# Linear attention and gated FFN: orders of their own for the first tile on three engines, casts of the value weights on GpSimd, a tiny first activation

## The chip, the cores and the metric

One core of a Trainium2 chip. The metric is the device time of one execution in microseconds (us), the median of several runs.

## The reference, cut

```python
x = _layernorm(x + attn(x, Wq, Wk, Wv, Wo))
x = _layernorm(x + ffn(x, ...))
# attn: x is 1 x 4096 x 512; 16 query heads, 4 key/value heads of 128
q, k = rope(x @ Wq.T), rope(x @ Wk.T); v = x @ Wv.T
qf, kf = elu(q) + 1, elu(k) + 1
# per head, over the sequence:
state = state + k_s[:, None] * v_s[None, :]; z = z + k_s
out = (q_s @ state) / (q_s . z + 1e-6);  out @ Wo.T
# ffn: Walsh-Hadamard transforms around gate/up (2048) and down, silu(gate) * up, scales
```

## The kernel before, in words

The program runs in three stages: attention over 8 tiles of 512 tokens, the output projection with the first norm over 32 chunks of 128, and the FFN. All products of float32 are made of three matmuls of upper and lower parts: `hi = round(x)`, `lo = x - hi`, and `hi*hi + hi*lo + lo*hi`. So each weight block and each operand needs an upper part (a copy, mostly on ScalarE) and a lower part (a subtraction, mostly on VectorE) before TensorE can use it.

In the attention stage each engine has a list of events written out by hand (`ORDER_PE`, `ORDER_ACT`, `ORDER_DVE`, `ORDER_POOL`, `ORDER_SP`); `events_in` reads them and `bodies` runs them in three places: "start" (the events marked with ', which belong to tile 0), a hardware loop over 7 tiles, and "end". An event is a letter, a key/value group g (0 to 3) and an index c:

- J (TensorE): projection of the key (c = 0) or query c of group g, 12 matmuls of 128x512, for all 512 tokens, into one of three banks `pj` that J, V, T and D share in turn. V: values of 128 tokens, 12 matmuls. T: transposes of the key features. D: denominators. C: scores of a chunk. U: numerators of a chunk. Z: the state's update.
- S (ScalarE): swaps the halves of J's result into `tb` (two instructions of 64x512). M (VectorE): result times cosines. I (GpSimd): `tb` times sines. R (VectorE): their sum. X (ScalarE): exponential. E (VectorE): the feature; it frees the bank of J. L: upper part of the feature on ScalarE (`Qh`) and lower part on GpSimd (`Ql`).
- W, K, A, N: upper parts on ScalarE and lower parts on VectorE of values, transposed keys, scores and state. G (GpSimd): the two causal selects on the scores' parts. H: parts of the x tile. Q (VectorE): running sum of the key features. P: query feature times that sum. O, Y: copies out of PSUM. B, S, O, Y on SyncE: loads of x and tables, stores.

In the first tile the weights come in too: 24 pieces of 128x512 (`piece`, in the order in which TensorE first uses them: J00 to J04, V0 to V3, J10 to J14, J20 to J24, J30 to J34). SyncE loads them one after the other (`load_piece`), `pieces_hi` makes the upper parts and counts them in `wa_hi`, `pieces_lo` makes the lower parts and counts them in `wa_lo`; TensorE's J or V waits for that count, and the first J of the second tile (J21) for all 24. Before, ScalarE makes all upper parts, and the table `ahead` says how many pieces are made ahead of each S on ScalarE and ahead of each M on VectorE: 3 ahead of the first, then 2 ahead of each of the next ten. TensorE waits by the order of the list: J02 needs E00 for its bank, J04 needs E01, V0 needs E02 and all four value pieces, J10 E03, V1 E04, J11 the lower part W1, J13 E10, J14 E11, V2 E12, V3 E13, and Z01 the lower part N01.

Of the kernel before, what the change touches and what calls it, by code (L numbers as in the profile page):

```python
# [10 lines left out]
ACT = mybir.ActivationFunctionType  # L11
# [77 lines left out]
NW = H + KV + DC  # L89
# [9 lines left out]
def jobs_before(kind, a, b, d, where):  # L99
# [15 lines left out]
                return found  # L115
    return found

LAST_PE = """  # L120
# [32 lines left out]
def phases(nc, xT, wq, wk, wv, cosT, sinT, x, wo, su, consts, wd, sd, wsd, wg, wu, wsg, wsu, num_d, den_d, rden_d, x1_d, x2_d, wd_d, out):  # L153
# [9 lines left out]
    with ctx:  # L163
        def sem(name):
            return ctx.enter_context(nc.semaphore(name))
# [134 lines left out]
        had_done = sem("had_done")  # L300
        had_free = sem("had_free")
        x2_out = sem("x2_out")
        f_in, sc_in, sd_ready = sem("f_in"), sem("sc_in"), sem("sd_ready")
        f_step, f_hi, f_lo, f_mm, f_w, f_out = sem("f_step"), sem("f_hi"), sem("f_lo"), sem("f_mm"), sem("f_w"), sem("f_out")
        w_in, wd_in = [sem(f"wc_in{i}") for i in range(XR)], [sem(f"wd_in{i}") for i in range(WDS)]
# [87 lines left out]
        order = list(first)  # L393
# [10 lines left out]

        def bodies(eng, name, body):

            body(-1, [e for e in EVENTS[name] if e[3] == 1], "start")
            with eng.Fori(0, NM - 1) as m:
                body(m, EVENTS[name], "middle")
            body(NM - 1, LAST_TILE.get(name, [e for e in EVENTS[name] if e[3] == 0]), "end")  # L410

        ahead = {(0, 0): 3}
        left = NW - 4
        for e in [e for e in EVENTS["ACT"] if e[0] == "S" and e[3]][1:]:
            ahead[e[1:3]] = min(2, left)
            left -= ahead[e[1:3]]
        assert left == 0

        def upto(m, d, per_tile, i):  # L420

# [291 lines left out]
        def _(act):  # L713
# [192 lines left out]
            def pieces_hi(n):  # L906
                for i in [next(pieces) for _ in range(n)]:
                    _, raw_w, hi, _ = piece(i)
                    act.wait_ge(wa_in[i], 16)
                    nc.scalar.activation(hi, raw_w, ACT.Copy).then_inc(wa_hi, 1)  # L910

            def body(m, events, where):
                for kind, g, c, d in events:
                    u = g * NCH + c
                    r = g * (G + 1) + c
                    if kind == "S" and where == "start":
                        pieces_hi(ahead.get((g, c), 0))
                    if kind == "S":
                        bank = pj[job_bank("J", g, c)]
                        act.wait_ge(j_done, upto(m, d, NR, r))  # L920
# [44 lines left out]
                    if where == "end":  # L965
                        between(kind, g, c)

            pieces = iter(range(NW))
            act.wait_ge(zeroed, 5)
            pieces_hi(1)  # L970
            bodies(act, "ACT", body)
# [14 lines left out]
        def _(dve):  # L986
# [225 lines left out]
            def pieces_lo(n):  # L1212
                for i in [next(pieces) for _ in range(n)]:
                    _, raw_w, hi, lo = piece(i)
                    dve.wait_ge(wa_hi, i + 1)
                    nc.vector.tensor_tensor(lo, raw_w, f32(hi), ALU.subtract).then_inc(wa_lo, 1)

            def body(m, events, where):
                for kind, g, c, d in events:
                    u = g * NCH + c  # L1220
                    r = g * (G + 1) + c
                    if kind == "M" and where == "start":
                        pieces_lo(ahead.get((g, c), 0))
                    if kind in "MRE":
                        bank = pj[job_bank("J", g, c)]
                    if kind == "M":
# [90 lines left out]
        def _(pool):  # L1317
# [66 lines left out]
            def row_root(k, t):  # L1384
                i = k * NCH + t
                pool.wait_ge(lnc_step, i * 3 + 3)
                nc.gpsimd.tensor_tensor(crstd[:, :], cve[:, :], neghalf[:, :], ALU.pow).then_inc(rc_done, 1)

            def body(m, events, where):
                for kind, g, c, d in events:  # L1390
                    u = g * NCH + c
                    r = g * (G + 1) + c
                    if kind == "I":
                        if r == 0:
                            pool.wait_ge(cs_in, m * 32 + (d * 32 + 32))
                        pool.wait_ge(shifted, upto(m, d, NR, r))
                        nc.gpsimd.tensor_tensor(tb[c][:, :], tb[c][:, :], sinb[:, :], ALU.mult).then_inc(sin_done, 1)  # L1397
                    elif kind == "L":
                        pool.wait_ge(hi_done, upto(m, d, NR, r))
                        nc.gpsimd.tensor_tensor(Ql[g % 2][:, c, :], (tb[c] if c else Kf)[:, :], f32(Qh[g % 2][:, c, :]),  # L1400
                                                ALU.subtract).then_inc(lo_done, 1)
                    elif kind == "G":
                        pool.wait_ge(sc_free, upto(m, d, NU, u))
                        nc.gpsimd.sem_inc(passed, 1)
                        for a in (Ah[u % 2], Al[u % 2]):

                            ins = nc.gpsimd.affine_select(out=a[:, :, :], in_=a[:, :, :], compare_op=ALU.is_ge, fill=0.0,  # L1407
                                                          base=0, pattern=[[0, G], [1, CH]], channel_multiplier=-1)
                        ins.then_inc(a_ready, 1)
# [3 lines left out]
            nc.gpsimd.memset(carry[:], 0.0).then_inc(zeroed, 1)  # L1413
            nc.gpsimd.memset(minus1[:], -1.0).then_inc(zeroed, 1)
            nc.gpsimd.memset(onesd[:], 1.0).then_inc(zeroed, 1)
            nc.gpsimd.memset(neghalf[:], -0.5).then_inc(zeroed, 1)

            for s, tile in ((j_done, NR), (v_done, NCH), (t_done, KV), (dn_done, KV), (shifted, NR), (cos_done, NR),
                            (sin_done, NR), (rot_done, NR), (exp_done, NR), (f_done, NR), (hi_done, NR), (lo_done, NR),
# [25 lines left out]
        def _(sp):  # L1445
# [171 lines left out]
                sp.dma_start(xst[:, c, :], xT[0, :, c, :]).then_inc(xst_in[c], 16)  # L1617
            sp.dma_start(pr[-1][:, :], xT[0, :, DC - 1, :]).then_inc(xst_in[DC - 1], 16)
            load_piece(1)
            sp.dma_start(cosb[:, :], cosT[:, 0:MT]).then_inc(cs_in, 16)  # L1620
            sp.dma_start(sinb[:, :], sinT[:, 0:MT]).then_inc(cs_in, 16)
            sp.dma_start(identb[:, :], consts[:, 0:P]).then_inc(c_in, 16)
            for i in range(2, NW):
                load_piece(i)
            sp.dma_start(had[:, :], consts[:, P:2 * P]).then_inc(mat_in, 16)
            bodies(sp, "SP", body)
# [109 lines left out]
```

## Time and profile before

| | us |
|---|---|
| median of 3 runs | 2312.55 (2310.44 to 2315.09) |
| the profiled execution | 2315.09 |
| its span | 2313.4 |
| TensorE busy | 2251.4 (97%) |
| VectorE busy | 1826.6 (79%) |
| ScalarE busy | 1274.0 (55%) |
| GpSimd busy | 1128.7 (49%) |

The profile is one execution on the chip. Its timeline rows give the start of an instruction, its time, engine, source line, operation, and in brackets how long the engine had been idle before it and what ended the wait. PE is TensorE, DVE VectorE, ACT ScalarE, POOL GpSimd, SPq the queue of SyncE.
### The profile page before, as it was taken

Reading aid. Unit: us, or ns where it says so; the run is one execution under the profiler, and the core shown is the slowest. Engines: PE = TensorE matmul, PEld = TensorE weight load, DVE = VectorE, ACT = ScalarE, POOL = GpSimd, SP = SyncE. Lnnn points to the kernel's source line nnn. Section 1 sums busy time; section 2 is a strip of 40 time slices with the busy share of each in tenths; the row PEclk is TensorE's granted clock in tenths of the full one; section 3 lists DMA queues with packets and bytes.
Section 4 is the critical chain, followed back from the end, with each engine's and each line's share of the span. In section 5 each row is a group of like instructions: output and inputs, shape, how many; then the busy total and the mean of one; then the engine's idle time right before and its main releaser. Section 6 shows DMA issues by size and latency. Waiting matters only on the chain.

```text
span 2313.4 us, 32819 instructions
## 1 busy us (share of the span) xinstructions
PE 2251.4 (97%) x10209; PEld 1820.0 (79%) x10209; DVE 1826.6 (79%) x2452; ACT 1274.0 (55%) x2285; POOL 1128.7 (49%) x1002
## 2 busy tenths in 40 slices
PE   7999999999999999899999989999999999999998
PEld 5778777787878786787777768888888888888886
DVE  7877777878686868687887896787888788878877
ACT  6666666666676767233334455454445554554543
POOL 4677677767676767355544633321242133303321
PEclk9999999999999999999999999999999999999999
DMA  4010111111020115677767541323233322222313
GB/s 154 36 65 37 68 37 68 51 49 68 32 73 32 68 71 190 235 250 251 248 229 262 190 139 62 123 78 114 78 100 94 116 85 94 91 82 82 104 61 101
DMA packets 132701, 252.75 MB, mean 109 GB/s; under 512 B 44576, under 2 KB 45344, under 8 KB 122880
## 3 DMA queue, kind: packets, MB, share of 16 engines
q1 hardware_dynamic: 132608, 251.60, 32.3%
q8 instruction: 48, 0.79, 0.1%
q14 instruction: 45, 0.37, 0.1%
HBM read 188.11 MB, written 63.44 MB: 109 GB/s over the span
## 4 chain that ended last, share of the span: by engine, by line
PE 70%; issue 11%; POOL 9%; DVE 6%; ACT 2%; DMA 1%; SPq 0%; POOLq 0%; ACTq 0%; DVEq 0%
PE pj L548 17%; PE pj L629 11%; PE pnum L629 6%; PE pj L643 5%; PE psc L629 5%; PE pst L629 4%; PE psc L643 4%; PE pj L558 3%; PE pnum L643 3%; PE psc L579 3%; PE pnum L597 3%; PE pnum L600 3%; PE pst L643 2%; POOL fa L1337 1%; PE pst L586 1%
## 5 line engine op out<-in xcount | busy, mean ns | idle before, releaser
L1364 POOL TENSOR_TENSOR wcs<-wcr 128x256 f32<-128x256 f32 x64 | 67.3, 1051 | 514.1 <-DVE wcl L1106 504.2
L1397 POOL TENSOR_TENSOR tb<-tb,sinb 128x512 f32<-128x512 f32 x160 | 224.3, 1402 | 91.5 <-ACT tb L925 90.7
L548 PE MATMUL pj<-xah,wqh 128*128 128x512 f32 x512 | 203.3, 397 | 4.4 <-DVE Kf L1242 2.7
L478 PE MATMUL pj<-woh,oh 128*128 128x512 f32 x512 | 202.8, 396 | 1.7 <-issue 1.7
L1400 POOL TENSOR_TENSOR Ql<-tb,Qh 128x512 fp32r<-128x512 f32 x128 | 170.5, 1334 | 68.8 <-ACT Qh L934 68.8
L478 PE MATMUL pj<-woh,ol 128*128 128x512 f32 x512 | 200.4, 391 | 0.0
L478 PE MATMUL pj<-wol,oh 128*128 128x512 f32 x512 | 200.2, 391 | 0.0
L548 PE MATMUL pj<-xal,wqh 128*128 128x512 f32 x512 | 200.2, 391 | 0.0
L548 PE MATMUL pj<-xah,wql 128*128 128x512 f32 x512 | 200.1, 391 | 0.0
L1230 DVE TENSOR_TENSOR pj<-pj,cosb 128x512 f32<-128x512 f32 x160 | 111.2, 695 | 69.1 <-ACT tb L925 68.5
L629 PE MATMUL pj<-xch,wch 128*128 128x512 f32 x384 | 150.2, 391 | 8.5 <-DVE xcl L1112 6.2
L924 ACT ACTIVATE tb<-pj 64x512 f32<-64x512 f32 x160 | 95.5, 597 | 112.7 <-PE pj L548 108.7
L1407 POOL TENSOR_SCALAR_AFFINE_SELECT Ah<-Ah 128x512 fp32r<-128x512 f32 x128 | 102.0, 797 | 109.8 <-DVE Al L1271 109.1
L629 PE MATMUL pj<-xcl,wch 128*128 128x512 f32 x384 | 149.4, 389 | 0.0
L629 PE MATMUL pj<-xch,wcl 128*128 128x512 f32 x384 | 149.4, 389 | 0.0
L1256 DVE TENSOR_TENSOR pr<-tb,zc 128x512 f32<-128x512 f32 x128 | 140.5, 1112 | 1.2 <-PE pj L572 1.2
L1234 DVE SCALAR_TENSOR_TENSOR pj<-pj,tb 128x512 f32<-128x512 f32 x160 | 110.9, 693 | 35.1 <-POOL tb L1397 33.8
L928 ACT ACTIVATE tb<-pj,minus 128x512 f32<-128x512 f32 x160 | 110.5, 691 | 44.2 <-DVE pj L1234 42.6
L1320 POOL TENSOR_TENSOR rstd<-ve,neghalf 128x1 f32<-128x1 f32 x32 | 48.6, 1520 | 174.5 <-DVE ve L1000 174.5
L548 PEld LDWEIGHTS pj<-xah,wqh 128*128 128x128 f32 x512 | 96.7, 189 | 32.3 <-issue 7.5
L1177 DVE SCALAR_TENSOR_TENSOR tha<-tha,ga 128x512 f32<-128x512 f32 x64 | 53.6, 838 | 80.8 <-ACT tha L869 80.6
L839 ACT ACTIVATE wdh<-wdr 128x512 fp32r<-128x512 f32 x123 | 77.1, 627 | 70.3 <-PE pj L643 34.8
(258 smaller groups left out, 7070.5 us busy)
## 6 DMA issues: line engine op xcount, KB each, us to landing
num_scratch<-no SPq DMA_DIRECT2D x128, 256.0 KB, 2.4
nt<-num_scratch SPq DMA_DIRECT2D x32, 1024.0 KB, 5.4
rb<-rden_scratch SPq DMA_DIRECT2D x32, 1024.0 KB, 6.3
wdr<-wd_scratch SPq DMA_DIRECT2D x128, 256.0 KB, 3.3
wcr<-in_wg SPq DMA_DIRECT2D x64, 256.0 KB, 2.8
wcr<-in_wu SPq DMA_DIRECT2D x64, 256.0 KB, 3.1
xst<-in_xT SPq DMA_DIRECT2D x34, 256.0 KB, 3.7
xr<-in_x SPq DMA_DIRECT2D x32, 256.0 KB, 5.6
```

The source lines that it names most:

```text
L478: last = nc.tensor.matmul(py[s][:, :], a[s][:, h, :], b[:, h, :], start=(h == 0 and i == 0), stop=(h == H - 1 and i == 2))
L548: last = nc.tensor.matmul(bank[:, :], w[:, b, :], x[:, b, :], start=(k == 0), stop=(k == 11))
L629: last = nc.tensor.matmul(bank[:, :], a[n % 2][:, w, c, :], b[i][:, c, :], start=(start and k == 0), stop=(k == 5), skip_group_check=True)
L643: last = nc.tensor.matmul(result_banks(k)[t][:, :], a[:, tok], b[:, :], start=(f == 0 and i == 0), stop=(f == FB - 1 and i == 2))
L924: nc.scalar.activation(tb[c][0:64, :], bank[64:128, :], ACT.Copy)
L928: nc.scalar.activation(tb[c][:, :], pj[job_bank("J", g, c)][:, :], ACT.Exp, bias=minus1[:, 0:1]).then_inc(exp_done, 1)
L1230: nc.vector.tensor_tensor(bank[:, :], bank[:, :], cosb[:, :], ALU.mult).then_inc(cos_done, 1)
L1234: nc.vector.scalar_tensor_tensor(out=bank[:, :], in0=bank[:, :], scalar=1.0, in1=tb[c][:, :], op0=ALU.add, op1=ALU.add).then_inc(rot_done, 1)
L1256: nc.vector.tensor_tensor(pr[c - 1][:, :], tb[c][:, :], zc[:, :], ALU.mult).then_inc(z_product, 1)
L1397: nc.gpsimd.tensor_tensor(tb[c][:, :], tb[c][:, :], sinb[:, :], ALU.mult).then_inc(sin_done, 1)
L1400: nc.gpsimd.tensor_tensor(Ql[g % 2][:, c, :], (tb[c] if c else Kf)[:, :], f32(Qh[g % 2][:, c, :]), ALU.subtract).then_inc(lo_done, 1)
L1407: ins = nc.gpsimd.affine_select(out=a[:, :, :], in_=a[:, :, :], compare_op=ALU.is_ge, fill=0.0, base=0, pattern=[[0, G], [1, CH]], channel ...
```

## The change

Three tables give ScalarE, VectorE and GpSimd orders of their own for the start body; the loop's orders stay. In them `wN` makes the next N pieces (upper parts on ScalarE, lower parts on VectorE), `vN` the next N upper parts of value weights on GpSimd, counted by a semaphore of their own. The table `ahead` is gone. TensorE's and SyncE's lists are the same, but the load of the third piece (J02) is issued ahead of the cosines. ScalarE's first instruction is an activation of one column that makes the constant -0.5 (a memset on GpSimd before) and waits for no load; the load of the activation table stands ahead of it.

```diff
+FIRST_DVE = """
+H0 H1 H2 H3 w2 M00 R00 w1 E00 M01 w1 R01 E01 M02 w1 R02 w3 E02 M03 R03 w1 Q0 E03 M04 R04 W0 E04 M10 w2 R10 W1
...
-            body(-1, [e for e in EVENTS[name] if e[3] == 1], "start")
+            body(-1, [e[:3] + (1,) for e in FIRST_TILE[name]] if name in FIRST_TILE else
+                 [e for e in EVENTS[name] if e[3] == 1], "start")
...
-                    if kind == "S" and where == "start":
-                        pieces_hi(ahead.get((g, c), 0))
+                    if kind == "w":
+                        pieces_hi(g)
...
-            pieces = iter(range(NW))
+            pieces = iter([i for i in range(NW) if order[i][0] != "V"])
+            act.wait_ge(zeroed, 4)
+            nc.scalar.activation(neghalf[:, :], minus1[:, 0:1], ACT.Copy, scale=0.5).then_inc(half_ready, 1)
             act.wait_ge(zeroed, 5)
...
-                    dve.wait_ge(wa_hi, i + 1)
+                    if order[i][0] == "V":
+                        dve.wait_ge(wv_hi, len([k for k in order[:i] if k[0] == "V"]) + 1)
+                    else:
+                        dve.wait_ge(wa_hi, len([k for k in order[:i] if k[0] != "V"]) + 1)
                     nc.vector.tensor_tensor(lo, raw_w, f32(hi), ALU.subtract).then_inc(wa_lo, 1)
...
+            def pieces_hi(n):
+                for i in [next(pieces) for _ in range(n)]:
+                    _, raw_w, hi, _ = piece(i)
+                    pool.wait_ge(wa_in[i], 16)
+                    nc.gpsimd.tensor_copy(hi, raw_w).then_inc(wv_hi, 1)
...
-            nc.gpsimd.memset(neghalf[:], -0.5).then_inc(zeroed, 1)
...
             load_piece(1)
+            load_piece(2)
             sp.dma_start(cosb[:, :], cosT[:, 0:MT]).then_inc(cs_in, 16)
...
-            for i in range(2, NW):
+            for i in range(3, NW):
                 load_piece(i)
```

VectorE in the first tile, from the projection J01 to E02; before (`wql<-rq,wqh`, `wvl<-rv,wvh`, `wkl<-rk,wkh` are lower parts of query, value and key weights; `tb_68` is of J02):

```order
L1234 SCALAR_TENSOR_TENSOR pj<-pj,tb_67 128x512
L1242 SCALAR_TENSOR_TENSOR tb_67<-tb_67,pj 128x512
L1216 TENSOR_TENSOR wvl<-rv,wvh 128x512 x2
L1230 TENSOR_TENSOR pj<-pj,cosb 128x512
L1234 SCALAR_TENSOR_TENSOR pj<-pj,tb_68 128x512
L1216 TENSOR_TENSOR wvl<-rv,wvh 128x512
L1216 TENSOR_TENSOR wkl<-rk,wkh 128x512
L1230 TENSOR_TENSOR pj<-pj,cosb 128x512
L1242 SCALAR_TENSOR_TENSOR tb_68<-tb_68,pj 128x512
```

The same place now:

```order
L1252 SCALAR_TENSOR_TENSOR pj<-pj,tb_67 128x512
L1260 SCALAR_TENSOR_TENSOR tb_67<-tb_67,pj 128x512
L1248 TENSOR_TENSOR pj<-pj,cosb 128x512
L1234 TENSOR_TENSOR wvl<-rv,wvh 128x512
L1252 SCALAR_TENSOR_TENSOR pj<-pj,tb_68 128x512
L1234 TENSOR_TENSOR wvl<-rv,wvh 128x512 x3
L1260 SCALAR_TENSOR_TENSOR tb_68<-tb_68,pj 128x512
```

The value pieces moved behind M02, three of them between R02 and E02; the key piece of J10 and M03 moved behind E02.

GpSimd in the same stretch, now (before, four sine products and lower parts `Ql` alternated here, and there was no `CAST`):

```order
L1425 TENSOR_TENSOR tb_67<-tb_67,sinb 128x512
L1411 CAST wvh<-rv 128x512
L1425 TENSOR_TENSOR tb_68<-tb_68,sinb 128x512
L1411 CAST wvh<-rv 128x512 x3
L1425 TENSOR_TENSOR tb_69<-tb_69,sinb 128x512
L1428 TENSOR_TENSOR Ql_64<-Kf,Qh_62 128x512
L1425 TENSOR_TENSOR tb_70<-tb_70,sinb 128x512
L1428 TENSOR_TENSOR Ql_64<-tb_67,Qh_62 128x512
```

The lower part of the key features moved behind the sine product of J03, and three casts stand between the sine products of J02 and J03.

ScalarE at the end of the first tile, before:

```order
L959 ACTIVATE Sh_90<-pst 128x128
L910 ACTIVATE wqh<-rq 128x512 x2
L924 ACTIVATE tb_66<-pj 64x512
L925 ACTIVATE tb_66<-pj 64x512
L943 ACTIVATE Kth<-pj 128x512
```

and now:

```order
L972 ACTIVATE Sh_90<-pst 128x128
L937 ACTIVATE tb_66<-pj 64x512
L938 ACTIVATE tb_66<-pj 64x512
L923 ACTIVATE wqh<-rq 128x512 x3
L956 ACTIVATE Kth<-pj 128x512
```

The last upper parts of weights moved behind S20 and are three instead of two; the transposed keys' upper part K1 stands behind them.

## Rows read from the trace of the kernel before

**Rows 1.** Busy time (instructions) by engine in stretches; then PEclk, DMA share, GB/s

```profile
core 0: us, PE busy (x) PEld busy (x) DVE busy (x) ACT busy (x) POOL busy (x), PEclk, DMA share, GB/s
0.00:80.00 80.00, 60.03 (x242) 45.78 (x242) 59.21 (x81) 50.15 (x89) 37.09 (x39) 0.96 0.33 117
80.00:200.00 120.00, 118.26 (x564) 94.80 (x565) 94.20 (x147) 80.58 (x150) 83.31 (x76) 1.00 0.15 54
200.00:320.00 120.00, 119.38 (x571) 95.81 (x570) 91.70 (x141) 81.47 (x150) 85.92 (x78) 1.00 0.14 48
```

**Rows 2.** Timeline of TensorE, first tile (start, us, instruction, idle before)

```profile
7.52 0.77 PE L548 MATMUL pj<-xah,wkh 128*128 128x512 f32 x1 [5.18 <-DVE xal L1268]
...
12.57 0.39 PE L548 MATMUL pj<-xah,wqh 128*128 128x512 f32 x1
...
18.12 0.50 PE L548 MATMUL pj<-xah,wqh 128*128 128x512 f32 x1 [2.66 <-DVE Kf L1242]
...
20.03 0.63 PE L548 MATMUL pj<-xah,wqh 128*128 128x512 f32 x1
...
32.33 0.50 PE L558 MATMUL pj<-wvh,xah 128*128 128x512 f32 x1 [4.16 <-DVE tb L1242]
...
44.83 0.51 PE L548 MATMUL pj<-xah,wqh 128*128 128x512 f32 x1 [0.57 <-DVE Vl L1259]
...
58.08 0.30 PE L586 MATMUL pst<-Vh,Kth 128*128 128x128 f32 x1 [3.08 <-DVE Sl L1276]
...
64.09 0.50 PE L558 MATMUL pj<-wvh,xah 128*128 128x512 f32 x1 [1.36 <-DVE tb L1242]
...
68.48 0.50 PE L558 MATMUL pj<-wvh,xah 128*128 128x512 f32 x1 [1.33 <-DVE tb L1242]
...
81.11 0.49 PE L548 MATMUL pj<-xah,wqh 128*128 128x512 f32 x1 [1.19 <-DVE wql L1216]
```

**Rows 3.** Timeline of ScalarE, its first instructions

```profile
4.05 1.28 ACT L910 ACT_TABLE_LOAD   x1 [4.05 <-DMA rk<-in_wk]
5.34 0.63 ACT L910 ACTIVATE wkh<-rk 128x512 fp32r<-128x512 f32 x1
...
8.17 0.63 ACT L950 ACTIVATE xah<-pr 128x512 fp32r<-128x512 f32 x1 [0.64 <-DMA pr<-in_xT]
...
13.26 0.60 ACT L924 ACTIVATE tb<-pj 64x512 f32<-64x512 f32 x1
```

**Rows 4.** The tile xst in the first 3 us: its loads, and their time to landing

```profile
L1617 SPq DMA_DIRECT2D xst<-in_xT x3: 417/431/440, 1.3 to 2.2; - x3
...
DMA to landing us min/median/max: 3.5/4.1/4.2
```

**Rows 5.** Timeline of VectorE, lower parts beside and without GpSimd

```profile
20.09 1.77 DVE L1216 TENSOR_TENSOR wvl<-rv,wvh 128x512 fp32r<-128x512 f32 x1
...
50.88 1.12 DVE L1216 TENSOR_TENSOR wkl<-rk,wkh 128x512 fp32r<-128x512 f32 x1
...
79.60 1.28 DVE L1216 TENSOR_TENSOR wql<-rq,wqh 128x512 fp32r<-128x512 f32 x2
```

**Rows 6.** Timeline of GpSimd, products with sines and selects

```profile
19.68 1.63 POOL L1397 TENSOR_TENSOR tb<-tb,sinb 128x512 f32<-128x512 f32 x1 [3.79 <-ACT tb L925]
...
26.33 1.30 POOL L1397 TENSOR_TENSOR tb<-tb,sinb 128x512 f32<-128x512 f32 x1 [3.33 <-ACT tb L925]
...
50.37 1.09 POOL L1407 TENSOR_SCALAR_AFFINE_SELECT Ah<-Ah 128x512 fp32r<-128x512 f32 x1
...
73.71 0.64 POOL L1407 TENSOR_SCALAR_AFFINE_SELECT Ah<-Ah 128x512 fp32r<-128x512 f32 x1 [0.77 <-DVE Al L1271]
```

**Rows 7.** Timeline of ScalarE, end of the first tile

```profile
75.96 0.59 ACT L924 ACTIVATE tb<-pj 64x512 f32<-64x512 f32 x1 [1.26 <-PE pj L548]
...
77.90 0.60 ACT L943 ACTIVATE Kth<-pj 128x512 fp32r<-128x512 f32 x1 [0.74 <-PE pj L566]
```

More of the change, by code:

```diff
@@ L116, in jobs_before @@
     return found
+FIRST_ACT = """
+H0 H1 H2 H3 w1 S00 w1 S01 w1 X00 w1 S02 X01 L00 S03 X02 L01 w1 S04 X03 L02 W0 X04 L03 L04 S10 w2 W1 X10 K0 A00
+N00 A01 L10 S11 w2 S12 w2 X11 N01 O00 L11 S13 w2 X12 N02 L12 S14 w3 X13 O01 L13 W2 X14 L14 W3 A02 A03 N03 S20 w3
+K1 N10
+"""
+FIRST_DVE = """
+H0 H1 H2 H3 w2 M00 R00 w1 E00 M01 w1 R01 E01 M02 w1 R02 w3 E02 M03 R03 w1 Q0 E03 M04 R04 W0 E04 M10 w2 R10 W1
+E10 K0 A00 N00 A01 P01 P02 P03 M11 w2 P04 R11 Q1 E11 N01 M12 w2 R12 M13 w2 E12 N02 R13 M14 w3 E13 R14 W2 E14 W3
+A02 A03 N03 Y0 P11 K1 M20 w3
+"""
+FIRST_POOL = """
+I00 I01 v1 I02 v3 I03 L00 I04 L01 L02 L03 L04 I10 G00 L10 G01 I11 I12 L11 I13 L12 I14 L13 L14 G02 G03 I20
+"""
+FIRST_TILE = {"ACT": events_in(FIRST_ACT), "DVE": events_in(FIRST_DVE), "POOL": events_in(FIRST_POOL)}
 LAST_PE = """
@@ L302, in phases @@
         x2_out = sem("x2_out")
+        half_ready, wv_hi = sem("half_ready"), sem("wv_hi")
         f_in, sc_in, sd_ready = sem("f_in"), sem("sc_in"), sem("sd_ready")
@@ L410, in bodies @@
             body(NM - 1, LAST_TILE.get(name, [e for e in EVENTS[name] if e[3] == 0]), "end")
[L413 to L418, printed above, removed]
         def upto(m, d, per_tile, i):
@@ L1221, in body @@
                     r = g * (G + 1) + c
-                    if kind == "M" and where == "start":
-                        pieces_lo(ahead.get((g, c), 0))
+                    if kind == "w":
+                        pieces_lo(g)
                     if kind in "MRE":
@@ L1387, in row_root @@
                 nc.gpsimd.tensor_tensor(crstd[:, :], cve[:, :], neghalf[:, :], ALU.pow).then_inc(rc_done, 1)
+            def pieces_hi(n):
[3 more added lines that the diff above has]
+                    nc.gpsimd.tensor_copy(hi, raw_w).then_inc(wv_hi, 1)
+            pieces = iter([i for i in range(NW) if order[i][0] == "V"])
             def body(m, events, where):
@@ L1392, in body @@
                     r = g * (G + 1) + c
+                    if kind == "v":
+                        pieces_hi(g)
                     if kind == "I":
@@ L1426, in _ @@
             pool.wait_ge(sc_in, 48)
-            pool.wait_ge(zeroed, 6)
+            pool.wait_ge(half_ready, 1)
             steps(pool, step)
```

## The prediction

> **What bounds the kernel now.** I read the windows first [rows 1]. From 80 us on TensorE is busy for 118.26 and 119.38 of each 120 us at full clock; a tile of the attention loop is its own matmuls and little else. In the first 80 us it is busy for 60.03. So the change, which touches that stretch alone, can move the end only by what it moves the first matmul of the second tile (J21): what TensorE does from there on is the same list, back to back. Next I read TensorE's own timeline of the first tile for the rows with an idle time in brackets [rows 2]: it stands still before the first product (until 7.52), J02 (2.66), V0 (4.16), J11 (0.57), Z01 (3.08), V2 (1.36), V3 (1.33) and J21 (1.19). Each but the first and last waits for an operand or a bank that VectorE frees. So the first tile is bound by the chain product, shift (S), rotation (M, I, R), exponential (X), feature (E), bank free, and later by VectorE's list itself.
>
> J21 starts at 81.11 because the last lower part of a weight ends just before [rows 2]. I follow the new order along these TensorE waits, and carry the shift against before.
>
> **Prices.** ScalarE: a 128x512 copy 0.63, a half of S 0.60 [rows 3]. VectorE: two lower parts take 1.28, so one per 0.60 where it has the way free [rows 5]. GpSimd: a product with the sines or a lower part 1.27 to 1.30; a one-input select 0.64 [rows 6]. The new casts of V0 to V3 on GpSimd have no row. They can be as short as the select, or as long as a two-input product (1.30); I take 0.60 each, the select's pace, since both read one input of the same size, and keep 1.30 as the other end.
>
> **The port.** VectorE's lower part of V0 at 20.09 took 1.77: GpSimd's product had started at 19.68 and ran to 21.31, and the lower part ended 0.55 later. At 50.88 a lower part took 1.12 beside a select that began at 50.37 and took 1.09, since it had itself waited for VectorE [rows 5, 6]. So of a lower part (two inputs from SBUF) and an instruction of GpSimd, one waits for the other's end, and they alternate. A lower part that meets a two-input product costs VectorE up to 1.85 instead of 0.60. The new order gives GpSimd four more instructions and packs its list there, so this decides the sum.
>
> The Trainium skill, "SBUF — State Buffer", section "Who interferes with whom", says the same of the chip: a VectorE instruction with two SBUF inputs and a GpSimd instruction that reads SBUF exclude each other for the whole instruction. The trace agrees (1.77 and 1.12 against 0.60). It speaks against moving the casts to GpSimd; without the rule the sum would be that of the first rival.
>
> **Step 1, to J02: +0.1.** The table load (1.28) now lies under the wait for the first weight, which ends at 4.05 [rows 3]. The upper part of the key weight goes from 4.05 to 4.7. The x chunks were issued from 1.3 to 2.2 and land 3.5, 4.1 and 4.2 later, near 4.76, 5.84 and 6.4 [rows 4]; the fourth is waited for at 8.17 as before [rows 3]. So the first upper x part starts at 4.8, its lower part ends at 6.13, and the first matmul starts near 6.27 instead of 7.52. J00 took 5.05 [rows 2], so it ends near 11.6. Then S00 (1.2) to 12.85, the upper part of J02 to 13.5; but I00 holds GpSimd from 12.9 to 14.2, so the lower part of J02, which now stands ahead of M00, ends at 14.75. M00 and R00 end at 16.15. S01 ended at 15.65, so I01 holds the port until 17.0; the lower part of J03, which now stands ahead of E00, ends at 17.55, E00 at 18.17, and J02 starts at 18.2 (before 18.12). Both weights' lower parts stand in the gain's way. Where J00 meets the full clock earlier, all of this is up to 0.7 earlier. The cover of the removed table load is the DMA wait; the moved load of J02's weight is one place earlier in the queue, the cosines one later, needed only at 14.7: nothing. The memset that goes and the tiny activation (one column; shorter than the 0.60 of 512, and ahead of 4.05) are hidden too.
>
> **Step 2, to V0: +0.3.** TensorE was idle 2.66 before J02, and some matmuls of J02 ran at the low clock (the row at 20.03: 0.63 instead of 0.39) [rows 2]; with an idle time near 4 us I assume it again. S02 ends at 24.05, 2.2 earlier than before. From there, on VectorE: E01, M02, the lower part of V0 (behind the second cast), R02 to 27.75, the lower part of V1 to 28.3, then I03 (1.27) gets the port, the lower part of V2, then L00 (1.27), the lower part of V3 to 31.9, E02 to 32.55. V0 starts at 32.6 (before 32.33). Uncontended the same list would end 2.8 earlier.
>
> **Step 3, to J11: +1.1.** M03, R03, the lower part of J10 (behind L01), the scan Q0 (1.28 in place of its old spot at 18.1, where VectorE had time), E03 to 36.95; J10 at 37.05, V1 near 39.85, each 0.3 later. The lower parts for J11 and J12 stood ahead of M10 and now stand between M10 and R10, where I10 holds the port from 42.2 to 43.5. They end at 44.65 and R10 and W1 follow: J11 at 45.95 (before 44.83).
>
> **Step 4, to Z01: +2.3.** Up to M11 the list is the same. Then two lower parts and P04 meet I11 and I12 (1.27 each) where before they met selects (0.6): 1.2 more.
>
> **Step 5, to V2: +2.2.** Four lower parts before E12 as before, again beside L11 and I13.
>
> **Step 6, to V3: +3.5.** Three lower parts instead of two stand behind M14, which waits for S14, which waits on ScalarE for L12; VectorE has 1.1 with nothing to do. E12 to E13 takes 5.65 instead of 4.4 [rows 2].
>
> **Step 7, to J21: +5.0.** Between V3 and J21 lay 12.63 [rows 2]. ScalarE now does three upper parts after S20 (75.96 in the old times) and ahead of K1, which stood at 77.90 [rows 7]: S20 1.2, three copies 1.65, so K1 ends 1.0 later, then VectorE does K1, M20 and three lower parts (1.9) where two stood ahead of M20. J21 comes 14.15 after V3: 1.5 more.
>
> **Sum.** +5.0, less 0.7 for the clock (half of step 1's 0.7, and some 0.35 where the low clock falls into the idle time): +4.3. The profiled execution took 2315.09 (span 2313.4 and 1.7 around it) and would take 2319.4; it was the slowest of three, 2.5 over the median of 2312.55. In terms of the median: **2316.8**. The uncertain casts (0.60 to 1.30) and ties on the port give 2314.6 to 2319.3 for this case. A measurement of this kernel can tell 0.2% (4.6 us) from no change, so this is mostly within it.
>
> **Rivals.** *The port hardly bites* (the casts and products slip between the lower parts). For it: lower parts at 79.60 ran at 0.64 apiece [rows 5]; against: GpSimd's list is dense just there. Then V0 comes 2.6 earlier, J11 to V3 3.6 earlier, and step 7 takes 1.5 back: 2312.55 - 2.1 = 2310.5. Chance 0.22. *The port bites at the start, the second half absorbs it*: the waits in steps 4 and 5 depend on who comes first by under 0.1 us; with those two gone the sum is 1.1 + 1.2 + 1.5 - 0.7 = +3.1, with step 3's also gone +2.0: near 2314.6. Chance 0.26. *GpSimd becomes the bound* (the slower side): if a cast takes 1.30, four of them are 2.8 more on a list that is full from S02 to I10, of which some 2 reach I10 and R10; so 2316.8 + 2.0 = 2318.8, slower by more than 4.6. It decides from about 0.8 per cast on. Chance 0.10. That the table load stays behind the first weight (the change doing less than it says) would cost nothing more, as step 1's gain is used up by J02 anyway; it goes with the others. Forecast: 0.42.
>
> The Trainium skill, "GPSIMD Engine Reference", section "Engine selection", calls one-input work on GpSimd roughly line-rate, which is against the last rival; no run here shows a cast yet.
>
> **Chances.** No case holds a gain of over 4.6 us: even with the port free, step 7 takes its part; 0.03. Slower by over 0.2%: nearly all of the last rival and about half of the forecast's upper half: 0.30. Within: 0.67. The range 2310.2 to 2319.2 reaches down to the first rival and up past the last.
>
> **What would show it.** The table load near 1.6 and the first matmul near 6.3; S00 near 11.7; lower parts of J02, J03 and V0 to V3 of over 1.1 us on VectorE beside GpSimd; casts of about 0.6; V0 not before 32; three upper parts between S20 and K1; J21 at 84 to 87. Casts of V0 to V3 with lower parts at 0.69 each and V0 near 30 would make it wrong, and so would J21 before 81.

## The result and the profile after

The changed kernel takes 2321.54 us, the median of 7 runs (2318.2 to 2321.96), where the kernel before, on the same chip, took 2312.74 (2310.44 to 2316.18, also 7). The ratio is 1.0029, 95% interval 1.0020 to 1.0038. The prediction said 2316.8, with 2310.2 to 2319.2 as its range and same as the likeliest case: the time lies 2.3 outside the range, on the side of slower. A second time, the same kernel took 2321.3 against 2313.33 (ratio 1.003, 1.0018 to 1.0041).

The runs of the changed kernel lie in two groups: three from 2318.2 to 2319.2 and four from 2321.5 to 2322.0. The profiled execution is one of the upper four; its span is 2319.8 (before 2313.4).

The windows of the changed kernel, to be read beside [rows 1] (stretch, busy time of each engine with its instructions, then the granted clock of TensorE, DMA share and GB/s):

```profile
0.00:20.00 20.00, 10.49 (x30) 7.81 (x31) 10.37 (x14) 10.10 (x16) 4.58 (x12) 0.93 0.89 314
20.00:40.00 20.00, 15.21 (x53) 11.64 (x53) 14.81 (x18) 9.39 (x16) 10.99 (x10) 0.81 0.35 126
40.00:60.00 20.00, 15.92 (x72) 12.24 (x70) 17.72 (x23) 12.51 (x24) 12.18 (x10) 1.00 0.00 1
60.00:80.00 20.00, 17.34 (x64) 13.79 (x65) 14.66 (x23) 12.60 (x23) 10.10 (x9) 0.83 0.07 27
80.00:100.00 20.00, 17.24 (x84) 13.18 (x83) 14.84 (x22) 11.72 (x22) 11.31 (x11) 1.00 0.07 27
```

J21 starts 6.39 later than before, and the span is 6.4 longer: the shift of the first tile reaches the end, as the prediction read it. One pair of traces says this only roughly. From J21 to the end the executions took 2233.98 before and 2234.04 here, 2234.85 when the changed kernel was traced again, and from 2231.3 to 2236.9 in the experiments below, whose code behind J21 is the same. New is the granted clock of 0.83 from 60 to 80 us, where it was 1.00 before. The rows of TensorE's timeline that answer to [rows 2] are, in this order, J00, J02, V0, J11, Z01, the first matmul of V3 and a later one, the first of what follows V3 (C02), J21, and the projection behind J21 (J22):

```profile
6.53 0.77 PE L561 MATMUL pj<-xah,wkh 128*128 128x512 f32 x1 [4.19 <-DVE xal L1286]
17.91 0.79 PE L561 MATMUL pj<-xah,wqh 128*128 128x512 f32 x1 [3.77 <-DVE Kf L1260]
32.79 0.79 PE L571 MATMUL pj<-wvh,xah 128*128 128x512 f32 x1 [4.78 <-DVE tb L1260]
46.16 0.50 PE L561 MATMUL pj<-xah,wqh 128*128 128x512 f32 x1 [0.71 <-DVE Vl L1277]
60.23 0.30 PE L599 MATMUL pst<-Vh,Kth 128*128 128x128 f32 x1 [3.17 <-DVE Sl L1294]
71.66 0.51 PE L571 MATMUL pj<-wvh,xah 128*128 128x512 f32 x1 [2.42 <-DVE tb L1260]
72.83 0.63 PE L571 MATMUL pj<-wvh,xah 128*128 128x512 f32 x1
76.11 0.40 PE L592 MATMUL psc<-Qh 128*128 128x512 f32 x1
87.50 0.49 PE L561 MATMUL pj<-xah,wqh 128*128 128x512 f32 x1 [2.76 <-DVE wql L1234]
93.37 0.44 PE L561 MATMUL pj<-xah,wqh 128*128 128x512 f32 x1
```

Before, V3 started at 68.48 [rows 2], and C02 followed at:

```profile
71.34 0.39 PE L579 MATMUL psc<-Qh 128*128 128x512 f32 x1
```

V3 took 4.45 (71.66 to 76.11), not 2.86 as before: eight of its matmuls read 0.60 to 0.63, which is the lower of TensorE's two levels, 1.2 GHz. Where the clock fell in the first tile is the thread of what follows, so here it is counted from the timelines, as the number of matmuls of 128x512 that read 0.59 to 0.63 (the first behind an idle time reads 0.5 to 0.8 and is not counted; J14's column has seven of J14 and the one behind it):

| kernel | J00 | J02 | V0 | J14 | V3 | behind J21 | in all |
|---|---|---|---|---|---|---|---|
| before | 9 | 7 | 7 | 0 | 0 | 0 | 23 |
| changed | 8 | 5 | 10 | 8 | 8 | 0 | 39 |

The start on ScalarE, to be read beside [rows 3], and then VectorE (the lower part of J02, that of J03, E01 behind an idle time, the lower part of V0, those of V1 to V3):

```profile
0.82 1.28 ACT L983 ACT_TABLE_LOAD   x1 [0.82 <-PEq L1743]
2.12 0.20 ACT L983 ACTIVATE neghalf<-minus 128x1 f32<-128x1 f32 x1
4.09 0.63 ACT L923 ACTIVATE wkh<-rk 128x512 fp32r<-128x512 f32 x1 [1.77 <-DMA rk<-in_wk]
11.43 0.60 ACT L937 ACTIVATE tb<-pj 64x512 f32<-64x512 f32 x1 [1.68 <-PE pj L561]
```

```profile
13.32 1.30 DVE L1234 TENSOR_TENSOR wql<-rq,wqh 128x512 fp32r<-128x512 f32 x1 [2.84 <-ACT wqh L923]
16.05 1.21 DVE L1234 TENSOR_TENSOR wql<-rq,wqh 128x512 fp32r<-128x512 f32 x1
24.25 0.69 DVE L1260 SCALAR_TENSOR_TENSOR tb<-tb,pj 128x512 f32<-128x512 f32 x1 [4.59 <-ACT tb L941]
25.46 1.07 DVE L1234 TENSOR_TENSOR wvl<-rv,wvh 128x512 fp32r<-128x512 f32 x1
27.05 5.09 DVE L1234 TENSOR_TENSOR wvl<-rv,wvh 128x512 fp32r<-128x512 f32 x3
```

And GpSimd beside them (the cast of V0, those of V1 to V3, the sines of J03, the lower part of the key features):

```profile
16.66 1.07 POOL L1411 CAST wvh<-rv 128x512 fp32r<-128x512 f32 x1
24.83 2.18 POOL L1411 CAST wvh<-rv 128x512 fp32r<-128x512 f32 x3
26.97 1.28 POOL L1425 TENSOR_TENSOR tb<-tb,sinb 128x512 f32<-128x512 f32 x1
28.21 1.71 POOL L1428 TENSOR_TENSOR Ql<-Kf,Qh 128x512 fp32r<-128x512 f32 x1
```

A cast takes 0.73 (2.18 / 3), near the 0.60 that was taken, and 1.07 for V0's, which ran beside a lower part of VectorE. The lower parts of V1 to V3 take 1.70 each in place of 0.60, since each lets an instruction of GpSimd through. By the Trainium skill, "SBUF — State Buffer", section "Who interferes with whom", a VectorE instruction with two SBUF inputs and a GpSimd instruction that reads SBUF exclude each other; the trace agrees (5.09 for three). And VectorE stood idle for 4.59 ahead of E01, right before it was short of time.

### The profile page after: what moved, and what is told of

Its sections match the earlier page's. It is cut to its first block, busy times and chain, and to the rows that moved or that the text cites. A ratio compares the mean times of both kernels' runs of the same rounds, so it can differ in the third digit from the quotient of the medians.

```text
span 2319.8 us, 32819 instructions
## 1 busy us (share of the span) xinstructions
PE 2257.9 (97%) x10209; PEld 1824.3 (79%) x10209; DVE 1828.9 (79%) x2452; ACT 1272.7 (55%) x2282; POOL 1131.8 (49%) x1005
## 4 chain that ended last, share of the span: by engine, by line
PE 71%; issue 11%; POOL 9%; DVE 6%; ACT 2%; DMA 1%; POOLq 0%; ACTq 0%; DVEq 0%; SPq 0%
PE pj L561 17%; PE pj L642 10%; PE pnum L642 6%; PE pj L656 5%; PE psc L642 5%; PE pj L571 4%; PE pst L642 4%; PE psc L656 4%; PE pnum L656 3%; PE psc L592 3%; PE pnum L610 3%; PE pnum L613 3%; PE pst L656 2%; POOL fa L1355 1%; PE pst L599 1%
```

## The experiments

J21 is the start of the second tile's first matmul in the profiled execution of each kernel. "Before" in a ratio is the kernel before, run on the same chip in the same rounds. Where no ratio is given, the kernel was run once.

### The start alone

```diff
 # kernel before, plus
+            nc.scalar.activation(neghalf[:, :], minus1[:, 0:1], ACT.Copy, scale=0.5).then_inc(half_ready, 1)
...
+            load_piece(2)
             sp.dma_start(cosb[:, :], cosT[:, 0:MT]).then_inc(cs_in, 16)
```

> The kernel before, with the tiny first activation and the earlier load of J02's weight alone; all orders as before. Theory (the new lists cost the time, the start gives nothing): the first matmul starts near 6.5 instead of 7.52, but ScalarE still makes the upper parts of J02 and J03 ahead of S00 and waits for their loads, so J02 starts within 0.7 of 18.1 and J21 within 1 us of 81.1; the time is within 2 us of before. Rival (the start's change itself does harm): J21 at 84 or later.

2312.88, ratio 0.9995 (0.9986 to 1.0005). The first matmul starts at 6.26 (before 7.52), J21 at 80.20 (before 81.11). The early start is real (0.9 at J21), and it buys nothing that can be measured in the time.

### The casts back on ScalarE

```diff
-w1 X00 w1 S02 X01
+w1 X00 w1 w4 S02 X01
-I00 I01 v1 I02 v3 I03 L00
+I00 I01 I02 I03 L00
```

> The changed kernel with the four upper parts of value weights back on ScalarE, in its idle time ahead of S02; the lower parts stay where they are. Theory (not the casts but the products I03 and L00 hold the lower parts of V1 to V3 up): the three lower parts between R02 and E02 still take over 3.5 us and V0 starts at 31.5 to 32.5 (after: 32.79). Rival (the casts on GpSimd are the cost): the three take about 2 us and V0 starts before 30.5.

2316.44 (J21 at 84.64). VectorE's lower parts of V1 to V3:

```profile
27.31 3.76 DVE L1231 TENSOR_TENSOR wvl<-rv,wvh 128x512 fp32r<-128x512 f32 x3
```

3.76 in place of 5.09: the casts cost VectorE 1.3 here. The other 2.0 over three free lower parts (3 x 0.60) comes from the sine product and the lower part `Ql` that GpSimd does anyway. So the casts are the smaller part, as was expected. V0 starts 1.06 earlier than in the changed kernel, J21 2.86 earlier: V3, behind the same idle time (2.44), ran at full clock in this execution, which is 1.6 of it. The time of the one execution is 5.1 lower; the other 2.2 lie behind J21, where the code is the same, and are not a gain of this edit.

### The lower part of the key features behind the sines of J04

```diff
-I02 v3 I03 L00 I04 L01
+I02 v3 I03 I04 L00 L01
```

> The changed kernel with one event of GpSimd's list moved: the lower part L00 behind the sine product I04. Theory (the port): one of the two two-input instructions beside the lower parts of V1 to V3 is gone, they take 3.3 to 4.2 instead of 5.09, and V0 starts at 31.0 to 31.9 instead of 32.79. Rival (VectorE is slow there for another reason, such as waiting for casts): V0 stays at 32.8.

2317.68 (J21 at 86.40). The three lower parts take 2.95 instead of 5.09, less than the 3.3 to 4.2 that was expected, so the product of GpSimd that moved away was what held them. V0 starts at 32.16 (from 32.79) and J10 at 37.81 (from 37.99). These starts understate the edit: all of J00 ran low in this execution, and J02 started at 19.16, 1.25 later than in the changed kernel; counted from J02, V0 comes 1.9 and J10 1.4 earlier. V3 (72.18, from 71.66) shows no gain. V3 was at full clock behind an idle time of 2.51, and J21, behind one of 2.76, was not.

### The last three pieces ahead of S20 and K1

```diff
-N03 S20 w3 K1 N10
+N03 w3 S20 K1 N10
-A02 A03 N03 Y0 P11 K1 M20 w3
+A02 A03 N03 w3 Y0 P11 K1 M20
```

> The changed kernel with the last three pieces ahead of S20 on ScalarE and ahead of Y0 on VectorE, where both engines are idle. Theory: V3 stays near 71.7, J21 comes 1.5 to 3 us earlier than 87.50 (TensorE's idle time of 2.76 ahead of it goes below 1), and the time falls by 1.5 to 3 us from the changed kernel's. Rival (the end of the tile is bound by K1 or D0, not by the pieces): J21 moves by less than 0.5.

2317.02, ratio 1.0012 (1.0003 to 1.0022), J21 at 82.89 and no idle time before it. J21 comes 4.6 earlier, of which 1.6 is V3 at full clock behind the same idle time (2.40) and 3.0 the two tables. The expectation had said 1.5 to 3, so it held for the tables and had no term for the clock. This is the largest single part of the loss: it lies in three upper and three lower parts that were put where ScalarE and VectorE are on the path. In the changed kernel, ScalarE and then VectorE stood so:

```profile
80.77 0.59 ACT L937 ACTIVATE tb<-pj 64x512 f32<-64x512 f32 x1 [2.30 <-PE pj L561]
81.98 1.68 ACT L923 ACTIVATE wqh<-rq 128x512 fp32r<-128x512 f32 x3
83.57 0.57 ACT L956 ACTIVATE Kth<-pj 128x512 fp32r<-128x512 f32 x1
85.38 1.88 DVE L1234 TENSOR_TENSOR wql<-rq,wqh 128x512 fp32r<-128x512 f32 x3
```

ScalarE had nothing to do for 2.30 before S20 and has the three upper parts behind it; the lower parts then end just before J21. In the experiment they lie ahead of S20:

```profile
76.66 1.67 ACT L923 ACTIVATE wqh<-rq 128x512 fp32r<-128x512 f32 x3
79.08 0.59 ACT L937 ACTIVATE tb<-pj 64x512 f32<-64x512 f32 x1 [0.74 <-PE pj L561]
77.45 3.22 DVE L1234 TENSOR_TENSOR wql<-rq,wqh 128x512 fp32r<-128x512 f32 x3
```

### The changed kernel again

> The changed kernel once more. Theory (the order sets TensorE's waits, the clock adds to them by chance): J11, Z01 and V3 within 1 us of 46.2, 60.2 and 71.7; whether the 12 matmuls of V3 run at 0.39 or 0.63 may differ, and J21 is near 87.5 with low clock there and near 85.9 without. Rival (the low clock at V3 belongs to the order): it is there again, J21 within 0.5 of 87.5.

2321.3, J21 at 87.67, seven matmuls of V3, seven of J14 and the one behind it at the low level: the places repeat in these two traces. That the order alone fixes them, as the rival has it, does not follow: with the last three pieces moved, the lists up to V3 are the same, V3 waited 2.40 too, and it ran at full clock.

### The value pieces in VectorE's idle time, alone and with the last three early

```diff
-I00 I01 v1 I02 v3 I03 L00
+I00 I01 v4 I02 I03 L00
-R01 E01 M02 w1 R02 w3 E02
+R01 w4 E01 M02 R02 E02
```

> The changed kernel with all four casts right behind the sine product of J01 on GpSimd and all four lower parts of values right behind R01 on VectorE, where both engines are idle for 5 us. Theory (the place beside I03 and L00 is the cost): the four lower parts take 2.4 to 3 us, V0 starts near 28 (TensorE's idle time before it under 0.5), J11 4 to 5 us earlier than 46.2, J21 3 to 5 us earlier than 87.5. Rival (E02 is bound by the chain S02, R02, X02, not by the lower parts): V0 after 31.

2319.02 (J21 at 82.14, J22 at 89.62).

```profile
20.37 2.48 DVE L1234 TENSOR_TENSOR wvl<-rv,wvh 128x512 fp32r<-128x512 f32 x4
```

Four lower parts take 2.48, and V0 starts at 28.46, 4.3 earlier. J21 comes 5.4 earlier, yet the time falls by 2.5 only: seven matmuls at the low level stand behind J21, so that J22 is only 3.75 earlier (89.62, from 93.37). The other 1.2 are lost behind J22, in code that is the same.

> Both edits together: values' casts and lower parts in the idle time, and the last three pieces ahead of S20 and Y0. Theory: the two gains add up, J21 at 78.5 to 81, so 0 to 2.5 us ahead of before (81.1), and the time within 3 us of before. Rival (VectorE's list from E10 on bounds V3 whatever comes ahead): J21 at 82 to 83, as with the second edit alone.

2312.55, ratio 0.9994 (0.9985 to 1.0003), J21 at 79.65: with both tables mended the change costs nothing that can be measured.

### Three new orders

```diff
+H0 H1 H2 H3 w2 M00 R00 w1 E00 M01 w1 R01 w2 E01 w2 Q0 w1 M02 R02 w1 E02 M03 w1 R03 E03 M04 w1 R04 W0 E04 M10 R10 W1
+E10 K0 A00 N00 A01 P01 P02 P03 w1 M11 P04 R11 Q1 E11 N01 M12 w2 R12 M13 w2 E12 N02 R13 M14 w2 E13 R14 W2 E14 w2 W3
+A02 A03 N03 w2 Y0 P11 K1 M20
```

(VectorE's; on ScalarE the upper parts likewise stand in its idle times, X01 goes ahead of S02 and X02 ahead of S03, and GpSimd casts all four value pieces behind I01 and makes L00 ahead of I03.)

> Orders of my own for the first tile: upper parts of J10 to J13 in ScalarE's idle time before S02, X01 ahead of S02, all casts and lower parts of values, the scan Q0 and the lower part of J10 in VectorE's idle time, X02 ahead of S03, the eleven remaining pieces spread so that none is behind S20. Theory (what is moved into idle time is gained until VectorE's full list from E10 on bounds): V0 near 28, J11 at 38.5 to 41, V3 at 61.5 to 65, J21 at 74 to 78, the time 3 to 7 us below before (2306 to 2310). Rival (the clock and the port take it back): J21 at 79 or later, the time within 2 us of before.

2310.83, ratio 0.9989 (0.9980 to 0.9998), J21 at 76.33. Faster than both kernels, by less than the 3 to 7 us that was expected, and by less than the trace of the one execution would say (its own time was 2308.22, the lowest of eleven).

### TensorE kept at work in its idle times

Here the question is the clock. Extra matmuls with no use stand where TensorE would wait; nobody reads what they write.

```diff
+                    if where == "start":
+                        for _ in range({("V", 3, 0): 9}.get((kind, g, c), 0)):
+                            nc.tensor.matmul(psc[0][:, :], xah[:, 0, 0:CH], xah[:, 0, :], start=True, stop=True)
```

> The changed kernel with nine more matmuls of 128x512 (upper x part by upper x part, into a score bank that nobody reads) between V2 and V3 of the first tile. At 0.23 each they take 2.05 of the 2.42 in which TensorE stood still there; the lists of the other engines are the same. Theory (part of the extra time is the clock: eight matmuls of V3 at 0.43 instead of 0.23, after TensorE had stood still): V3 starts at 71.7 as before, all its matmuls read 0.39, C02 comes 2.9 behind it instead of 4.4, J21 at 85.9 instead of 87.5, span 2318.2, time 2319.5 to 2320. Rival (VectorE's and ScalarE's lists set J21, the low clock lies under them): V3 at full clock but J21 at 87.5 and 2321.5. Second rival (the low clock comes from what TensorE did before V2): V3's matmuls read 0.63 all the same.

2320.67, ratio 1.0025 (1.0015 to 1.0034). The nine extra matmuls, V3, and then J21:

```profile
69.54 2.20 PE L547 MATMUL psc<-xah 128*128 128x512 f32 x9
72.15 0.50 PE L574 MATMUL pj<-wvh,xah 128*128 128x512 f32 x1 [0.41 <-DVE tb L1263]
...
86.37 0.79 PE L564 MATMUL pj<-xah,wqh 128*128 128x512 f32 x1 [2.78 <-DVE wql L1237]
86.95 0.63 PE L564 MATMUL pj<-xal,wqh 128*128 128x512 f32 x1
...
93.69 0.44 PE L564 MATMUL pj<-xah,wqh 128*128 128x512 f32 x1
```

V3 runs at full clock and J21 comes 14.22 behind it; the prediction had said 14.15 without the clock. But the low level then stands behind J21 (six matmuls; J22 comes 7.32 later, not 5.87). So the first theory holds for V3 and J21 and fails for the time.

With twelve more ahead of Z01 (`("Z", 0, 1): 12`):

> As the kernel with fillers ahead of V3, and twelve more ahead of Z01, where TensorE stood still for 3.17 (2.75 of it filled). Theory of the clock: J14 runs at full clock too (in the changed kernel eight of its matmuls read 0.63, in the kernel before none); its result is 1.5 earlier for S14 and M14, and as E13 waits for M14, V3 starts up to 1.5 earlier, J21 at 84.4 to 85.9, time 2318 to 2320. Rival (VectorE's own list, the lower parts ahead of E12, sets V2 and V3): J14 is faster, V3 stays at 71.7, and the kernel equals the one with fillers ahead of V3 alone.

2321.05, ratio 1.0027 (1.0016 to 1.0038). The first matmuls behind the idle time, those of J14 among them:

```profile
60.92 0.30 PE L602 MATMUL pst<-Vh,Kth 128*128 128x128 f32 x1 [0.49 <-DVE Sl L1297]
...
62.72 0.40 PE L564 MATMUL pj<-xah,wqh 128*128 128x512 f32 x1
```

J14 ran at full clock, and V3 starts at 72.36 where it had started at 72.15: the rival is right, J14's low clock lies beside the path, and VectorE's list sets V3. Six matmuls behind J21 read 0.63 again.

With nine ahead of V3 and ten ahead of J21:

> The changed kernel with nine extra matmuls ahead of V3 (as before) and ten more at the end of the start body, where TensorE stands still for 2.76 ahead of J21 (into a numerator bank that is free, 2.3 of the 2.76). With V3 alone filled, V3 to J21 took 14.22 at full clock (the prediction: 14.15), and six matmuls at the low clock stood behind J21 instead. Theory (the time over the prediction's order part is one low stretch, wherever the last long idle time puts it): none at V3, none behind J21; J21 14.2 behind V3, J22 5.9 behind J21; the times lose the upper cluster of 2320.2 to 2322.1 and gather at 2317.5 to 2319.5. Rival (the low stretch is by chance off the path): the median stays at 2320.7 to 2321.5.

2317.98, ratio 1.0023 (1.0014 to 1.0032).

```profile
83.15 2.43 PE L623 MATMUL pnum<-xah 128*128 128x512 f32 x10
86.10 0.49 PE L564 MATMUL pj<-xah,wqh 128*128 128x512 f32 x1 [0.52 <-DVE wql L1240]
```

V3 to J21 14.23, J21 to J22 5.85, and nine of the eleven runs from 2316.05 to 2319.6 (two lie above, at 2320.78 and 2321.68). The median is 3.5 under the changed kernel's. One low stretch is 1.5 to 1.6 in the traces. Of the 2.9 between the two profiled executions (2318.66 and 2321.54), 1.4 is J21 (86.10, from 87.50), and 1.5 lies behind it, in code that is the same; so the difference of the medians is not all the clock at V3 and J21.

With all of the idle times of the first tile filled (12 ahead of the first product, 14 ahead of J02, 18 ahead of V0, 12, 4, 9 and 10 ahead of Z01, V2, V3 and J21):

> The changed kernel with extra matmuls in every idle time of TensorE in the first tile: 12 of zeros ahead of the first product, 14 ahead of J02, 18 ahead of V0, 12 ahead of Z01, 4 ahead of V2, 9 ahead of V3, 10 ahead of J21. It answers to the kernel before with the same filled (2313.03, J21 at 81.70, 7 matmuls at the low clock), so the two differ by the orders alone. Theory (the prediction's order part of +5.0 is right, its clock term of -0.7 is what was wrong): J21 at 86.3 to 87.2, and 2317.5 to 2319 against 2313.0. Rival (the orders cost more than 5.0 and the clock nothing): 2320.5 to 2321.5.

2315.52, ratio 1.0009 (1.0000 to 1.0018), J21 at 83.75. No matmul of the first tile is left at the low level:

```profile
0.00:20.00 20.00, 17.41 (x62) 12.97 (x63) 10.31 (x14) 9.96 (x16) 4.61 (x12) 1.00 0.89 307
20.00:40.00 20.00, 18.26 (x78) 13.96 (x77) 15.18 (x19) 11.52 (x20) 13.28 (x11) 1.00 0.37 133
```

V0, J10, V3 and J21:

```profile
31.11 0.50 PE L574 MATMUL pj<-wvh,xah 128*128 128x512 f32 x1 [0.77 <-DVE tb L1268]
35.09 0.50 PE L564 MATMUL pj<-xah,wkh 128*128 128x512 f32 x1 [0.96 <-DVE tb L1268]
69.52 0.50 PE L574 MATMUL pj<-wvh,xah 128*128 128x512 f32 x1 [0.60 <-DVE tb L1268]
83.75 0.49 PE L564 MATMUL pj<-xah,wqh 128*128 128x512 f32 x1 [0.52 <-DVE wql L1242]
```

The time is 6.0 under the changed kernel, more than either theory said. In the traces 3.75 of it is J21; the other 2.3 lie behind J21, where nothing was filled, and why is open. By the Trainium skill, "TensorE: Matmul & The Clock Gate", section "Part 1: The HAM clock gate (the "warmup" mystery)", the low rate is the default and activity releases it; the trace agrees, as with work in every idle time the granted clock was 1.00 in each 20 us (0.81 to 0.93 in three of five without).

The kernel before with its idle times filled (12, 10, 15, 11, 4 and 4 ahead of the first product, J02, V0, Z01, V2 and V3):

> The kernel before plus extra matmuls in TensorE's idle times and nothing else: 12 of zeros ahead of the first product, 10 ahead of J02, 15 ahead of V0, 11 ahead of Z01, 4 each ahead of V2 and V3. In the kernel before 9, 7 and 7 matmuls of J00, J02 and V0 read 0.63. Theory of the clock: these 23 at 0.2 are worth 4.6, of which the part on the path (J00 all, J02 and V0 about half) is 2.5 to 3.5: J21 at 78, time 2309 to 2310.5. Rival (idle times take it up): J21 at 81, 2312.5; or the extra matmuls end too late and cost time: over 2313.

2313.03, ratio 0.9996 (0.9987 to 1.0005), J21 at 81.70: nothing. J00 ran at full clock in 2.87 instead of 5.05, and then ScalarE, which has two upper parts ahead of S00, waited for a load:

```profile
12.47 1.27 ACT L915 ACTIVATE wqh<-rq 128x512 fp32r<-128x512 f32 x2 [2.84 <-DMA rq<-in_wq]
13.77 0.60 ACT L929 ACTIVATE tb<-pj 64x512 f32<-64x512 f32 x1
```

J02 started at 18.61 (before 18.12) and kept its seven slow matmuls; V0's seven were gone, but J10 came 4.39 behind V0 (before 4.44), as it waits for E03.

The three new orders with their idle times filled, first without V0, V2 and V3 and then with them:

> The kernel with three new orders (pieces where VectorE and ScalarE stand idle, 2310.83) plus extra matmuls that keep TensorE at work in its idle times: 12 of zeros ahead of the first product, 14 ahead of J02, 3 ahead of J10, 4 ahead of V1, 9 ahead of Z01. Theory of the clock: the stretches at the low clock at J00 (5 matmuls), J02 (12) and J14 (12) go, worth 0.2 each, 1 + 2.4 + 2.4; what lies on the path of it is at least 3, so J21 at 73.3 or earlier instead of 76.33, time 2307 to 2308.5. Rival (the chain over VectorE takes the gain): J21 within 1 of 76.33, 2310 to 2311.

2309.17, ratio 0.9980 (0.9971 to 0.9989), J21 at 76.45, six matmuls of V0 at the low level.

> The kernel with three new orders and extra matmuls, with nine more ahead of V0 (TensorE stood still for 2.37 there and six matmuls of V0 read 0.63 after it), four ahead of V2 and seven ahead of V3. Theory (a low stretch on the chain to J21 costs about 0.2 for each matmul): V0 at full clock, J10 up to 1.3 earlier, J21 at 75.2 to 76.4, no matmul at 0.63, time 2307.5 to 2309. Rival (with these orders the pieces of the weights set J21, and the clock is off the path): J21 at 76.4 and 2309 to 2310.

2308.97, ratio 0.9979 (0.9970 to 0.9988), J21 at 76.20, none at the low level. Both are the fastest kernels here, but the extra matmuls hardly moved J21 (76.33 without; at 73.3 or earlier was expected of the first), and the intervals with and without them overlap: that they help these orders is not shown. In both, V0 waits for E02 behind VectorE's list.

## Why the prediction was wrong

Its steps, as the shift of a start against before, beside what the profile after showed. The last column is the changed kernel with all idle times filled against the kernel before filled in the same way. In the latter seven matmuls of J02 still read 0.63, which favours this column by up to 1.4 from V0 on.

| step | predicted | measured | filled |
|---|---|---|---|
| 1, J02 | +0.1 | -0.2 | -1.1 |
| 2, V0 | +0.3 | +0.5 | -1.8 |
| 3, J11 | +1.1 | +1.3 | -1.4 |
| 4, Z01 | +2.3 | +2.2 | -0.6 |
| 5, V2 | +2.2 | +2.3 | -0.8 |
| 6, V3 | +3.5 | +3.2 | +0.5 |
| 7, J21 | +5.0 | +6.4 | +2.1 |
| clock | -0.7 | in the rows above | |

**Steps 1 to 6** came out within 0.3. At two of them this is in part luck. J02 started 3.8 behind J01's end, so it follows J00's clock, and in the traces of the changed kernel and its variants that leave J00 as it was it lies anywhere from 17.21 (five low matmuls in J00) to 19.16 (all behind its first); by V3 most of that is gone (71.60 to 72.36 where VectorE's order up to there is the same). And V2 had no idle time before it: J14's low matmuls held TensorE until then, not VectorE's list as step 5 has it; with J14 at full clock V2 waited for VectorE (1.10) and came 5.81 behind Z01 instead of 6.12. The lower parts of J02 and J03 stood in the early start's way (1.30 and 1.21 apiece; TensorE waited 3.77 ahead of J02, and 3.07 in the start alone, which has the orders of before; S00 started at 11.43, 1.8 earlier than before, and J02 only 0.2). The casts took 0.73 (1.07 for V0's), and the lower parts took 1.07 (V0) and 5.09 (V1 to V3) beside GpSimd.

**The clock term of the sum failed, and with it the time from V3 to J21.** V3 to J21 is 15.84 in the trace, before 12.63. Of the 3.2 more, 1.6 is the order, as predicted (1.5; with V3 at full clock it is 14.22 and 14.23 in two kernels), and 1.6 is V3 at the low level, which the prediction did not have. It subtracted 0.7 because a faster start and longer idle times would hide low stretches; no row stood behind either half of that figure. The sign was wrong. Step 6 itself makes V3 wait 2.42 and step 7 makes J21 wait 2.76, where they had waited 1.33 and 1.19; in both traces of the changed kernel V3 then ran low, in four of its variants J21 did instead, and in one (casts back) neither. Nine extra matmuls ahead of V3 and ten ahead of J21 took both stretches away. Each is 1.5 to 1.6 on the chain (V3 to J21 15.84 against 14.22; J21 to J22 7.32 or 7.48 against 5.87). With +5.0 and +1.6 in place of +5.0 and -0.7 the sum is +6.6; the trace has +6.4.

**The step from one execution to the median** was the other half of the miss. The sum gave 2319.4 for an execution like the profiled one and took 2.5 off, as that had been the slowest of three; the median of seven runs of the kernel before was 2312.74, so its distance was real. The profiled execution after took 2321.54 (2.1 more than 2319.4, the clock), and this was the median itself, so nothing was to be taken off. Between the medians lie 8.8 (8.0 the second time), of which the first tile explains 6.4; the rest stays open. So does whether the two groups of runs (3.3 apart) are executions with and without low stretches: one stretch is 1.6, and no execution of the lower group has a trace. The granted clock of whole executions leans that way (0.994 to 0.995 in the lower three, 0.992 to 0.994 in the upper four), but executions also differ behind J21: from 1300 to 1400 us the clock was 1.00 before and 0.98 in both traces of the changed kernel, in code that is the same.

**What the steps had not seen.** They were right with the low clock at J02 and V0 in them, since step 2 assumed it at J02. Filled, the orders cost 2.1 at J21 and 2.5 in the time (2315.52 against 2313.03); filling took 3.75 off J21 and 6.0 off the changed kernel's time. The kernel before has 23 slow matmuls, nominally 4.6 at 0.2 each, and gets nothing that can be measured back when 16 of them go: J00's lie under the load that ScalarE waits for, V0's under J10's wait for E03. In the changed kernel those at J02, V0, V3 or J21 lie on the chain, because the order took the waits beside them away: S02 now starts with the end of J02 (22.31), where before it stood behind an exponential and two upper parts (25.06, J02 having ended at 22.73), and J10 comes 5.20 behind V0 and 3.98 when filled (4.44 and 4.39 in the kernel before). So a stretch costs by where it stands and not by its length alone.

**The rivals.** *The port hardly bites*: no, 5.09 for three. *The second half absorbs it*: no, +2.7 from V0 to V3, as forecast (+3.2). *GpSimd becomes the bound*: no, a cast is 0.73, under its point of 0.8. Its price of 2318.8 was closest to the time, but by another mechanism. The upper end of the range stopped at 2319.2 because none of the cases held a loss by the clock, though the timeline showed 23 slow matmuls behind idle times and the forecast lengthened the waits at V3 and J21. (The chance of 0.30 for slower is also not the sum it is given as: nearly all of 0.10 and half of the forecast's upper half, 0.105, is 0.2.)

## What to carry to other kernels

When a change makes TensorE wait longer in a place, ask whether what follows is on the chain; if so, put a low stretch there (here 1.5 to 1.6) into the range with its own chance, and never book a gain on the clock without a place for it. The same wait may bring the low level in one execution and not in another, so this is a chance and not a fixed cost. Work that fills an engine's list belongs where that engine's own idle time in the trace is (VectorE's 4.59 ahead of E01, ScalarE's 2.30 ahead of S20): the new orders, which move pieces there, turned a loss of 0.3% into a gain of 0.1%. Work out the sum for the profiled execution, and give its distance from the median a chance of its own instead of subtracting it.

## What was not expected of the hardware

- Matmuls on zeros raised the granted clock too: twelve of them ahead of the first product took 4.80 to 5.20, and no matmul of J00 behind them read more than 0.50 (0.63 without them).
- The same idle time led to either level: ahead of V3 the matmuls ran low behind 2.42 and 2.40 and at full clock behind 2.40, 2.44, 2.50 and 2.51; ahead of J21, behind 2.76 to 2.78, they ran low in four traces and full in three; Z01 waited 3.08 in the kernel before and 3.07 in the start alone, and J14 behind it ran at full clock in the one and low in the other.
- Three lower parts on VectorE took 1.88 with no instruction of GpSimd beside them, and 2.95, 3.22, 3.76 or 5.09 beside its selects, products and casts.
- With the same code behind J21, the executions took from 2231.3 to 2236.9 from there to the end (1.6 of the highest is a low stretch at J21 itself), a spread near the shift that was to be measured.
